# Cross-attention: the mask is put into the score banks by four 64x64 identity matmuls instead of two full ones

## The reference

```python
qh = (q @ Wq.T + bq).reshape(B, S, H, D_K).transpose(0, 2, 1, 3)      # H = 16 heads, D_K = 8
kh = (k @ Wk.T + bk).reshape(B, -1, H, D_K).transpose(0, 2, 1, 3)
scores = jnp.einsum('bhqd,bhkd->bhqk', qh, kh) / np.sqrt(D_K)
scores = jnp.where(mask, scores, -1000000000.0)
weights = jax.nn.softmax(scores, axis=-1)
out = jnp.einsum('bhqk,bhkd->bhqd', weights, vh)
```

## Time and profile before

| | us |
|---|---|
| device time, median of 3 runs (lowest, highest) | 864.27 (864.03, 864.41) |
| span of the profiled execution, first to last instruction | 857.5 |
| median less span (the page has no other time of the profiled execution) | 6.8 |
| TensorE busy, whole span | 713.5 (83%) |
| VectorE busy | 657.5 (77%) |
| ScalarE busy | 578.5 (67%) |
| GpSimd busy | 477.1 (56%) |
| L1208, busy in 214 recorded matmuls of 256 | 69.4 |

### The profile page before, as it was taken

One profiled execution on the slowest core, in us unless ns is written; L12 is line 12 of the kernel. 1 busy time (PEld: TensorE's weight loads), 2 busy tenths in 40 slices (PEclk: granted clock), 3 DMA queues, 4 the chain that ended last, 5 costly groups with the idle time before them and its releaser, 6 DMA issues.

```text
span 857.5 us, 16692 instructions
## 1 busy us (share of the span) xinstructions
PE 713.5 (83%) x5462; PEld 474.6 (55%) x5504; DVE 657.5 (77%) x1662; ACT 578.5 (67%) x747; POOL 477.1 (56%) x578
## 2 busy tenths in 40 slices
PE   3435688797898786999999999999994399999996
PEld 1124455464565553554444444444342399999994
DVE  4669999999899899788788898888745255555554
ACT  2513899999999989245666766657562267777771
POOL 2134887967966797424232634645354366566663
PEclk9855555555555555659999999999997599999999
DMA  9980000000000300051050100000015222222228
GB/s 297 336 274 0 1 1 1 1 0 1 2 1 1 75 0 1 1 157 44 24 169 19 39 25 27 15 17 23 14 33 166 75 60 82 77 79 76 79 79 270
DMA packets 56868, 56.63 MB, mean 66 GB/s; under 512 B 9712, under 2 KB 49520, under 8 KB 56656
## 3 DMA queue, kind: packets, MB, share of 16 engines
q1 hardware_dynamic: 51728, 45.14, 17.9%
q0 software_dynamic: 5056, 10.43, 3.7%
HBM read 25.97 MB, written 29.57 MB: 65 GB/s over the span
## 4 chain that ended last, share of the span: by engine, by line
PE 54%; DVE 24%; issue 12%; POOL 3%; DMA 3%; ACT 2%; SPq 1%; DVEq 0%; POOLq 0%; ACTq 0%
PE ops L1232 7%; PE slot L1337 6%; DVE S_FB L1467 5%; PE slot L1208 5%; DVE S_YZ L1479 4%; PE bps L1350 4%; PE slot L1216 4%; PE ops L1350 4%; PE slot L1045 4%; PE ops L1068 3%; DVE X_junk L1530 3%; DVE S_YZ L1500 3%; PE tps L1194 3%; PE bps L1082 2%; PE bps L1124 1%
## 5 line engine op out<-in xcount | busy, mean ns | idle before, releaser
L606 POOL TENSOR_TENSOR S_YZ<-S_YZ 128x512 f32<-128x512 f32 x128 | 183.0, 1463 | 56.1 <-ACT S_YZ L810 55.9
L861 ACT ACTIVATE B_W<-slot 128x1024 f32<-128x1024 f32 x128 | 131.3, 1026 | 92.5 <-PE slot L1216 92.4
L1530 DVE CUSTOM_DVE_ANT_0 X_junk<-tps,X_MB 128x512 bf16<-128x512 f32 x240 | 156.2, 688 | 31.7 <-PE tps L1194 30.9
L759 POOL DMA_INDIRECT picks<-F_ROUT,F_GOAL x94 | 103.0, 1096 | 70.9 <-DVE F_ROUT L1877 50.2
L1045 PE MATMUL slot<-S_UQT,S_UKT 32*128 32x256 f32 x256 | 84.9, 477 | 52.9 <-DVE S_YZ L1479 52.1
L1045 PEld LDWEIGHTS slot<-S_UQT,S_UKT 32*128 32x128 f32 x256 | 56.7, 298 | 83.2 <-DVE S_YZ L1479 68.7
L1467 DVE TENSOR_SCALAR S_FB<-slot 128x512 f32<-128x512 f32 x128 | 84.6, 684 | 18.5 <-PE slot L1049 18.0
L725 POOL DMA_INDIRECT rows<-B_ROW,B_IDX x64 | 62.7, 980 | 50.3 <-DVE B_ROW L1601 24.2
L1479 DVE SCALAR_TENSOR_TENSOR S_YZ<-slot,S_FB 128x512 f32<-128x512 f32 x128 | 83.5, 683 | 1.9 <-DVE S_FB L1467 0.5
L1049 PE MATMUL slot<-S_GQT,S_GKT 32*128 32x256 f32 x256 | 84.8, 447 | 0.0
L1194 PE MATMUL tps<-X_KFT,X_QFT 24*128 24x512 f32 x240 | 78.7, 519 | 3.4 <-DVE X_MX L1530 1.1
(11 more groups left out here) (300 smaller groups left out, 1595.9 us busy)
## 6 DMA issues: line engine op xcount, KB each, us to landing
rows<-S_blank SPq DMA_DIRECT2D x17, 1040.0 KB, 12.4
F_RIN<-rows SPq DMA_DIRECT2D x47, 130.0 KB, 2.1
B_W<-w1T SPq DMA_DIRECT2D x16, 256.0 KB, 4.4
F_W<-w2T SPq DMA_DIRECT2D x16, 256.0 KB, 4.9
X_CT<-ctxT SPq DMA_DIRECT2D x8, 256.0 KB, 4.7
B_W<-picks SPq DMA_DIRECT2D x8, 256.0 KB, 8.9
B_W<-picks SPq DMA_DIRECT2D x4, 384.0 KB, 5.6
picks<-F_ROUT,F_GOAL POOLq DMA_INDIRECT x94
```

Of the source, the lines that this page charges most:

```text
L606: g.tensor_tensor(Y[:, n % YR], Y[:, n % YR], Zr[:, n % ZR], ALU.add).then_inc(f_rdy, 1)
L861: act.activation(W[:, at:at + 2, 2 * j:2 * j + 2, :].rearrange("p h t n -> p h (t n)"), E_BANKS[k % 2][:, :, :], ACT.Exp, scale=SCALE).the ...
L1530: dve.tensor_tensor_reduce(out=junk[:, i, :], in0=bank, in1=MB[:, c % 2, t, :], scale=1.0, scalar=-3.0e38, op0=ALU.add, op1=ALU.max, accum ...
```

## The change

`MBR` is a new buffer like `MBT`, with the two halves of the partitions swapped: partitions 0 to 63 of `MBR` are 64 to 127 of `MBT`, and the other way round. SP's new function `mask_halves(c)` fills it by two DMA transfers of 64 partitions x 2 KB, after it has waited for `mbt_rdy`. It is called for c - 2 behind the transposed mask's load in round c, and for the last two batches behind the loop. A padding buffer `apart` of 288 floats a partition is taken out.

In a step, the two identity matmuls of 128 rows and 128 columns become four of 64 rows and 64 columns: bank 0 is fed from partitions 0 to 63 (its lower half from `MBT`, its upper half from `MBR`), bank 1 from partitions 64 to 127. Each streams 512 columns. In the first step of a batch TensorE also waits for both transfers (`turned_in`).

```diff
         MBT = sB("MBT", [2, TM, N], BF16)
+        MBR = sB("MBR", [2, TM, N], BF16)
...
-        sX("apart", [288])
...
+        turned_in = [sem(f"turned_in{i}") for i in range(2)]
...
+            def mask_halves(c):
+
+                p = c % 2
+                sp.wait_ge(mbt_rdy, c + 1)
+                for lo, hi in ((0, 64), (64, 0)):
+                    sp.dma_start(MBR[lo:lo + 64, p], MBT[hi:hi + 64, p]).then_inc(turned_in[p], 16)
...
                     sp.dma_start(MT8[:, p], mT_t[c]).then_inc(mt_in[p], 16)
+                    mask_halves(c - 2)
...
+            mask_halves(B - 2)
+            mask_halves(B - 1)
             sp.wait_ge(*t_emptied("proj", B - 1))
...
                 if hs == 0:
                     pe.wait_ge(mbt_rdy, b + 1)
+                    pe.wait_ge(turned_in[p], 32 * (b // 2 + 1))
...
-                for i in range(2):
-                    pe.matmul(E[:, i, :], ident_bf[:, :], MBT[:, p, 2 * j:2 * j + 2, :].rearrange("p t n -> p (t n)"),
-                              start=True, stop=False)
+                for i, at in enumerate((0, 64)):
+                    for to in (0, 64):
+                        src = MBT if to == at else MBR
+                        pe.matmul(E[to:to + 64, i, :], ident_bf[at:at + 64, at:at + 64],
+                                  src[at:at + 64, p, 2 * j:2 * j + 2, :].rearrange("p t n -> p (t n)"),
+                                  start=True, stop=False)
```

## The result

The changed kernel took 859.8 us in the median of 20 runs, the kernel before 864.3 us beside it: ratio 0.9944, 95% interval 0.9922 to 0.9965. The ratio is one of means and leaves out the changed kernel's three longest runs, 866 to 873 us; with all 20 it is 0.9962. A second comparison, with both on another occasion, gave 0.9963 (0.9937 to 0.9989). A third, on another chip, gave the opposite: 1.0171 (1.0130 to 1.0212), 922 us (6 runs) against 905 (17 runs). So the change gained about half a per cent in the first two comparisons and cost 1.7% in the third, where the granted clock was down for longer. 861.3 was forecast.

A forecast was written before the change was run, and what follows sets the result against it. TensorE was taken to bound cross-attention, with VectorE close behind. Terms of -4.7 (steps), -0.6 (steps at the lower clock), +0.3 (copies) and +2.0 (later clock rises) sum to -3.0 us: 861.3 us in the median, range 858 to 862.5.

The forecast's parts named there:

- Bound and place: Only the 128 cross-attention steps change; TensorE bounds them, VectorE is close behind and sets the pace in some.
- The streaming: In each step's mask, four 64x64 matmuls run together and stream for 0.21 us instead of 0.43.
- The switch: Ahead of each mask, after a full-array item ending every step, changing to 64x64 parts adds 0.09 us.
- The load: Behind the added switch, the new mask matmuls' weight loads expose 0.05 us a step; four starts add 0.02.
- How much of it counts: In cross-attention, 70% of TensorE's saving of 0.053 us a step counts, 4.7 us over 128 steps.
- The copies: At cross-attention's start, TensorE waits 0.3 us for the first pair of mask copies, bounds 0 to 1 us.
- A wait for the copies in a batch's first step: Sign that the forecast is wrong: TensorE waiting for the copies at any batch's first step; no size given.
- The clock: In cross-attention, rises at 383 and 410.2 come later, some 7 us more at the lower level, 2.0 us lost.
- The sum: Whole kernel: 3.0 us gained, 854.5 us for the span and 861.3 for the median.
- The clock stays down: Rival, cross-attention: less full-array work leaves the clock low 30 to 60 us more; 868 to 877 us, chance 0.30.
- The parts don't run together: Rival, mask matmuls: parts with the same rows take turns, 18 us slower, 882 us; chance 0.05.
- no switch: Rival, mask: no switch and no exposed load, 0.21 us saved a step, 849 to 854 us; chance 0.07.

The follow-up runs named there:

- `after_again`: The changed kernel, unaltered, run and profiled again as a control; ratio to the kernel before 0.9963.
- `col_halves`: The kernel before with each full mask matmul cut into two of 128 rows and 64 columns, no copies; ratio to the kernel before 1.0032.
- `next_steps`: Changed kernel with parts only in eight steps of batches 1 to 6 and all of batch 7, full matmuls elsewhere, no batch 0 copy; ratio to before 1.0033.
- `next_other`: Changed kernel with parts only in the eight steps of batches 1 to 6 that `next_steps` leaves out, full matmuls elsewhere; batch 1 took 34.09 us.
- `early_copy`: The changed kernel with the first copy issued ahead of the first loads of W1; ratio to the kernel before 0.9990.
- `b0_full`: The changed kernel with two full mask matmuls and no copy in batch 0, four parts in batches 1 to 7; ratio to the kernel before 0.9996.

## Why the prediction was right

**Bound and place.** Right: TensorE and VectorE share the pace of cross-attention, and outside of it the profiles moved by 0.7 us (the end of self-attention) and 1.4 us (the experts), neither of which `after_again` repeats.

**The streaming.** Right: the four parts run together. From the first to L1231 it is 0.34 us, which leaves 0.21 to 0.23 for the stream beside the switch behind it and the exposed load.

**The switch.** Right: 0.09 to 0.10 us, in the changed kernel and in `col_halves`, and nothing in the nine steps where the array changed its form anyway. That every step ends with an item on the full array was wrong for these nine.

**The load.** Mis-sized: 0.02 us exposed instead of 0.05, and the four starts took 0.01 instead of 0.02. So the step saves 0.09 to 0.10 us of TensorE's time and not 0.053.

**How much of it counts.** Mis-sized the other way: a steady batch is 0.72 us shorter, half of 16 x 0.09, so the share that counts is 0.50 and not 0.70. The mask's share of the chain says how much of its time lies on the path today; VectorE was close enough behind to take the path over in some of the steps. `next_steps` and `next_other` show that 8 of 16 steps carry most of it, and `col_halves`, with half of its cost passed on, gives the same share in the other direction. The two errors pull against each other and nearly cancel: 0.037 us a step forecast, 0.045 measured in a steady batch. With the last two batches, which gain more, batches 1 to 7 gave 6.0 us where the forecast had 4.7 for all eight. The step of the argument that I would now put otherwise is this product of a well-read duration with a share of a chain.

**The copies.** Mis-sized: 0.3 forecast, 1.7 measured (2.67 of idle time less the 0.96 that stood there before), above the upper bound of 1. A wait for the copies in a batch's first step was also named as a sign of being wrong, and it came, in batch 0. I had let them land 3 to 4 us after the issue at 370.1; the pair was issued from 370.74 to 371.9 and waited for at 377.6. That `early_copy`, with the pair ahead of the W1 loads, starts at 375.59 shows that their place in the queue was the cause.

**The clock.** The forecast had a rise a few us late and 2.0 us lost. The rise came 11 us late (8.5 us more at the lower level, counted from the first mask matmul). Steps 3 to 5 of batch 0 grew by 0.39, 1.34 and 0.56 us, 2.3 in all, and the batch by 1.4, which is just what the forecast's -0.6 and +2.0 come to. The price of 0.3 us for each us at the lower level held: 0.35 in the long fall of `b0_full`, about 0.33 on the last chip.

**The sum.** The forecast was 3.0 us; the spans differ by 3.6 and the medians by 4.5. That it came so close is in part luck. The copies were 1.4 us too cheap and the steps 1.3 us too small, and these cancel. The 0.7 us of self-attention and the 1.4 us of the experts were in no forecast. `after_again`, which has neither, gives 2.7.

**The rivals.** "The clock stays down" was put at 0.30 and 868 to 877 us. It did not happen in the profile of the first comparison, it happened in part in two variants on the chip of the second, and it happened in full on another chip, 17 us slower. The forecast and this rival are both true of the same program. I had asked on which side of the edge the kernel stands, and had not asked what moves it across: there, it seems, stalls that are none of the change's doing. In the kernel before, three stalls over 2 us, at 492.5, 567.4 and 605.5, are each followed within some 4 us by a fall of 3.4 us; in the changed kernel the five falls last 6.8, 13.7, 10.3, 6.9 and 27.3 us. The 10, 17, 21 and 65 us for none, half, half and all of the steps, and the late rise in the table above, both speak for the mask's missing full-array work as what keeps it down; that stalls differ from execution to execution leaves it short of shown. "The parts don't run together" and "no switch" are refuted by the rows above.

## What to carry to other kernels

A cheaper form of work on TensorE pays only in the steps where no other engine is about to take over; read those from the differences of two traces, and mind which step's work an interval holds. Cutting matmuls into parts of the array saves streaming, but paid a switch of 0.09 to 0.10 us here at each added change of form, and none where the form changed already. Taking full-array work away, in parts or altogether, also doubled the time until the clock came up here: look at the granted clock of several executions, and on more than one chip, before you believe half a per cent.

## What the runs showed of the hardware

- Four 64x64 bf16 matmuls, two of them on the same rows and two on the same columns, start within 0.01 us; from there to the next form's first matmul it is 0.34 us, against 0.52 for two full matmuls.
- The added switch costs 0.10 us: the step saves 0.10 behind a full-array item and 0.20 behind a product on column parts, where no switch is added.
- A 64-column bf16 load on a 64x64 part takes 103 ns, a full 128-column one 98. Behind a switch the first exposes 0.02 us, a 128-column fp32 load 0.10.
- TensorE busy for all of 10.8 us, and the clock at 0.50 (1.2 GHz) throughout and beyond [the stretch 383 to 393.8 above]: being busy was not enough. Without any mask matmul the clock came up as late as with the parts (14.8 us against 14.9 to 16.2).
- The same kernel took 859 to 867 us on one chip and 899 to 908 on another, with batch 1 the same to 0.02 us (34.29 and 34.27).
- Self-attention, untouched, ended in two ways: its last maxima matmuls start at 372.9 to 373.7 us in 8 profiles and at 377.6 to 378.7 in 6, with the clock at 0.50 for most of it. Both kinds occur with and without the change.
